# Softmax exponentials turned by 64x64 matmuls with the identity, one PSUM bank per batch element

## The chip, the cores and the metric

The kernel runs on one core of one Trainium2 chip. The metric is the device time of one execution in microseconds; lower is better. The kernel before takes 2504.32 us, the median of three runs (2503.06 to 2508.76).

## What is computed

Four layers of attention run over x, 64 batch elements of 64 tokens by 256 features, in float32. Layer 0 is a gated memory attention. Layers 1 and 3 are the same block: rotary self attention (16 heads of 16 features, causal, weights chosen per token from two experts), cross attention to a context of 64 tokens by 128 features (16 heads of 8), and a gated feed forward with two experts. Layer 2 is a latent attention (16 heads of 64, masked keys) with a GELU feed forward. What matters here is the same line in three of them:

```python
scores = jnp.einsum('bhqd,bhkd->bhqk', q * scale, k)
p = jax.nn.softmax(scores.astype(jnp.float32), axis=-1)
return jnp.einsum('bhqk,bhkd->bhqd', p, v)
```

The exponentials come out with the queries on the partitions. The product with the values contracts over the keys, so they have to be turned: keys on the partitions, for every head and batch element.

## The kernel before, in words

The 64 batch elements are worked on in 32 pairs (PAIRS). A tile `x_tile(p)` has 128 rows: 64 tokens (S) of each of the two elements of pair p. The layers are phases that follow one another. In each phase every engine has its own block with its own list of instructions, written out by hand as a loop over pairs that is shifted by one to three pairs from one step to the next. Semaphores order the engines: `x_ok.at(p + 1)` is the count at which pair p is done, and `at(p)` the count for the pair before. There is no scheduler.

PSUM is one tensor `ps_all` of eight banks of 512 columns: `ps_a`, `ps_b`, `ps_t` (0, 1, 2), `ps_s` (3 and 4), and `ps_p`, `ps_o`, `ps_d` (5, 6, 7).

For pair p, the exponentials are `probs[:, u]`, 128 partitions (64 queries of two elements) by 1024 columns (16 heads by 64 keys). In all three phases they are turned like this:

- **TensorE** makes eight transpositions of 128x128 (`probs_t` in self attention, L1005, and in cross attention, L1401; `prob_transposes` in latent attention, L551). Four go to bank `ps_p`, four to `ps_d`, and each four are announced by one step of `pt_pe`. A turned block has two heads by 64 keys on the partitions and two elements by 64 queries in the columns.
- **ScalarE** copies each bank into `pt` (`pt_copy`, L1123 and L1488; `prob_copies`, L561), 128x512 each, as soon as its own four blocks are done.
- **TensorE** multiplies with the values in `pv` (L1021 in self, L1415 in cross, L1786 in latent attention).

The order of the steps on TensorE in one round of the loop:

- self attention: scores(p), dense(p-2), probs_t(p-1), proj_qk(p+2), pv(p-1), xt_(p+3), proj_v(p+2), out_t(p-1), qk_t(p+2). The scores (L991) and pv are 64x64 float32 matmuls, and dense (L1037 to L1039) and proj_qk (L946 to L948) are full-array ones with 512 columns.
- cross attention: scores(p) (L1389, 64x64 with 512 columns), probs_t(p-1), proj_qk(p+2) (L1362, L1364), out_t(p-2) (L1423), proj_v(p) (L1376), xt_(p+3) (L1352), pv(p-1), dense(p-2) (L1431).
- latent attention: scores(p) (L1758 with a mask, then L1766: 32 matmuls of 64x64 with 64 columns, in all four quadrants of the array), half of a projection of a later group (L1720 to L1722), prob_transposes(p-1), the other half, keys (L1732 to L1734), pv(p-1), values (L1746), dense(p-1).

In cross attention ScalarE's round is pt_copy(p-1), qkt_copy(p+2) (L1480), ot_copy(p-2) (L1504), xt_copy(p+3), the two exponentials of p (L1497), and a statistic. Outputs and their transposition share bank `ps_o`, so pv(p-1) waits for ot_copy(p-2):

```python
pe.wait_ge(pt_ok.handle, pt_ok.at(p + 1))
pe.wait_ge(v_ok.handle, v_ok.at(p + 1))
if ot_ok.due(p):
    pe.wait_ge(ot_ok.handle, ot_ok.at(p))
```

Bank `ps_d` has a second user in two phases: in self attention qk_t (its copy is counted by `qkt_ok`), in latent attention dense (its reader is counted by `res_ok`).

Of the kernel before, what the change touches and what calls it, by code (L numbers as in the profile page):

```python
# [43 lines left out]
J = NH // 2  # L44
# [63 lines left out]
def build(nc, t):  # L108
    with ExitStack() as ctx:
# [421 lines left out]
        def softmax_norm(pool, sm, probs, p, u):  # L531
# [2 lines left out]
            nc.gpsimd.tensor_tensor(pr, pr, sm[:, u, 1].unsqueeze(2).broadcast_to([P, NH, S]), ALU.mult) \  # L534
                .then_inc(prob_ok.handle, 1)

        def prob_transposes(pe, probs, p, u):

            pe.wait_ge(prob_ok.handle, prob_ok.at(p + 1))
            for r, bank in enumerate((ps_p, ps_d)):  # L540

                if r == 0:
                    if pt_ok.due(p):
                        pe.wait_ge(pt_ok.handle, pt_ok.at(p))
                    if o_ok.due(p):
                        pe.wait_ge(o_ok.handle, o_ok.at(p))
                else:
                    if res_ok.due(p):
                        pe.wait_ge(res_ok.handle, res_ok.at(p))
                for j in range(4):  # L550
                    ins = nc.tensor.transpose(bank[:, j * P:j * P + P],  # L551
                                              probs[:, u, (4 * r + j) * P:(4 * r + j + 1) * P], ident)
                ins.then_inc(pt_pe.handle, 1)

        def prob_copies(act, pt, p):
            for r, bank in enumerate((ps_p, ps_d)):
                act.wait_ge(pt_pe.handle, pt_pe.at(p, r + 1))
                if r == 0:
                    if pv_pe.due(p):
                        act.wait_ge(pv_pe.handle, pv_pe.at(p))  # L560
                nc.scalar.activation(pt[:, 4 * r:4 * r + 4].rearrange("p j q -> p (j q)"), bank[:], ACT.Copy) \  # L561
                    .then_inc(pt_ok.handle, 1)


# [310 lines left out]
        def self_attention(n, loaded, load_next):  # L875
            with ExitStack() as own:
# [27 lines left out]
                pt = ob("pt", [P, J, P])  # L904
# [11 lines left out]
                with nc.Block() as block:  # L916
# [10 lines left out]
                    def _(pe):  # L927
# [67 lines left out]
                                ins.then_inc(s_pe.handle, 1)  # L995

                        def probs_t(p):
                            for r, bank in enumerate((ps_p, ps_d)):
                                pe.wait_ge(exp_ok.handle, exp_ok.at(p, r + 1))
                                if r == 0 and on_ok.due(p):  # L1000
                                    pe.wait_ge(on_ok.handle, on_ok.at(p))
                                if r == 1:
                                    pe.wait_ge(qkt_ok.handle, qkt_ok.at(min(p + 3, PAIRS)))
                                for j in range(4):
                                    ins = nc.tensor.transpose(bank[:, j * P:j * P + P],  # L1005
                                                              probs[:, p % 2, (4 * r + j) * P:(4 * r + j + 1) * P], ident)
                                ins.then_inc(pt_pe.handle, 1)

                        def pv(p):

                            pe.wait_ge(pt_ok.handle, pt_ok.at(p + 1))
                            wait_slot(pe, p)
                            if o_ok.due(p):
                                pe.wait_ge(o_ok.handle, o_ok.at(p))
                            for j in range(J):
                                at = 4 * (j % 4 // 2) + 2 * (j // 4) + j % 2
                                for h in range(2):
                                    rows = slice(S * h, S * h + S)
                                    for b in range(2):
                                        v = (v_own if b == h else v_swap)[rows, p % VS, 2 * j + h]  # L1020
                                        ins = nc.tensor.matmul(o_at[b * S:b * S + S, h, j], pt[rows, at, b * S:b * S + S], v,  # L1021
                                                               start=True, stop=True, skip_group_check=True)
                            ins.then_inc(pv_pe.handle, 2)

# [49 lines left out]
                    def _(act):  # L1074
# [43 lines left out]
                        def pt_copy(p):  # L1118
                            for r, bank in enumerate((ps_p, ps_d)):
                                act.wait_ge(pt_pe.handle, pt_pe.at(p, r + 1))  # L1120
                                if r == 0 and pv_pe.due(p):
                                    act.wait_ge(pv_pe.handle, pv_pe.at(p))
                                nc.scalar.activation(pt[:, 4 * r:4 * r + 4].rearrange("p j q -> p (j q)"), bank,  # L1123
                                                     ACT.Copy).then_inc(pt_ok.handle, 1)

                        def out_high(p):
# [183 lines left out]
        def cross_attention(n, loaded, load_next):  # L1310
            with ExitStack() as own:
# [18 lines left out]
                pt = ob("pt", [P, J, P])  # L1330
# [5 lines left out]
                with nc.Block() as block:  # L1336
# [9 lines left out]
                    def _(pe):  # L1346
# [46 lines left out]
                                ins.then_inc(s_pe.handle, 1)  # L1393

                        def probs_t(p):
                            for r, bank in enumerate((ps_p, ps_d)):
                                pe.wait_ge(exp_ok.handle, exp_ok.at(p, r + 1))
                                if pt_ok.due(p):
                                    pe.wait_ge(pt_ok.handle, pt_ok.at(p - 1, r + 1))
                                for j in range(4):  # L1400
                                    ins = nc.tensor.transpose(bank[:, j * P:j * P + P],  # L1401
                                                              probs[:, p % 2, (4 * r + j) * P:(4 * r + j + 1) * P], ident)
                                ins.then_inc(pt_pe.handle, 1)

                        def pv(p):

                            if p == 0:
                                pe.wait_ge(cold.handle, cold.at(0, 2))
# [4 lines that stand above are left out]
                            for j in range(J):  # L1413
                                for b in range(2):
                                    ins = nc.tensor.matmul(ps_o[b * S:b * S + S, j * 2 * HV:(j + 1) * 2 * HV],  # L1415
                                                           pt[:, j, b * S:b * S + S],
                                                           vb[:, p % 2, b, j].rearrange("p h d -> p (h d)"),
                                                           start=True, stop=True, skip_group_check=True)
                            ins.then_inc(pv_pe.handle, 2)
# [39 lines left out]
                    def _(act):  # L1459
# [23 lines left out]
                        def pt_copy(p):  # L1483
                            for r, bank in enumerate((ps_p, ps_d)):
                                act.wait_ge(pt_pe.handle, pt_pe.at(p, r + 1))
                                if r == 0 and pv_pe.due(p):
                                    act.wait_ge(pv_pe.handle, pv_pe.at(p))
                                nc.scalar.activation(pt[:, 4 * r:4 * r + 4].rearrange("p j q -> p (j q)"), bank,  # L1488
                                                     ACT.Copy).then_inc(pt_ok.handle, 1)

                        def exp_(p):
# [148 lines left out]
        def latent_attention(loaded, load_next):  # L1640
            with ExitStack() as own:
# [23 lines left out]
                pt = ob("pt", [P, J, P])  # L1665
# [25 lines left out]
                with nc.Block() as block:  # L1691
# [9 lines left out]
                    def _(pe):  # L1701
# [71 lines left out]
                        def pv(p):  # L1773
# [6 lines left out]
                            for r, bank in enumerate((ps_o, ps_p)):  # L1780
                                for j in range(4):
                                    for b in range(2):
                                        for h in range(2):
                                            rows = slice(S * h, S * h + S)
                                            at = (2 * j + r) * HD2
                                            ins = nc.tensor.matmul(  # L1786
                                                bank[rows, j * P + b * S:j * P + b * S + S],
                                                vb[p % 2][b][rows, at:at + HD2],
                                                pt[rows, 4 * r + j, b * S:b * S + S], start=True, stop=True,
                                                skip_group_check=True)  # L1790
                                ins.then_inc(pv_pe.handle, 1)

# [809 lines left out]
```

## Time and profile before

| | |
|---|---|
| median of three runs | 2504.32 us |
| the profiled execution | 2509.57 us |
| its span, first to last instruction | 2507.8 us |
| busy: TensorE (PE), its weight loads (PEld) | 2311.2 us (92%), 1890.0 us (75%) |
| busy: VectorE, ScalarE, GpSimd | 1410.7 us (56%), 1143.7 us (46%), 653.1 us (26%) |
| mean granted TensorE clock | 0.960 of 2.4 GHz |

A busy time is that of one engine, and engines overlap, so the column doesn't add up to the span. TensorE's instructions also overlap each other: a group's time is best read from the start of its first instruction to the start of the next group. "A <-B" names what is written and what is read, and "xN" the number of records merged into a row. PE is the matmul, PEld the load of its stationary operand, DVE is VectorE, ACT ScalarE, POOL GpSimd.

### The profile page before, as it was taken

The page shows a single profiled execution, that of the slowest core. Times are in us where ns is not written, and L with a number is a line of the kernel's source. Part 1 is how long each engine was busy: PE and PEld are TensorE (multiplying, and loading weights), DVE is VectorE, ACT ScalarE, POOL GpSimd, SP SyncE. Part 2 cuts the span into 40 slices and gives each one's busy share as a digit, 9 for nine tenths or more (in the row PEclk, how much of TensorE's full clock was granted, in tenths as well). Part 3 has the DMA queues.
Part 4 walks back from the last instruction along what each step waited for, and adds up shares of the span by engine and source line. Part 5 has one row for each costly group of instructions (what it writes and reads, how often), then busy time and mean ns, then how long its engine had stood idle before and what let it go on. Part 6 is the DMA issues. An engine that isn't in the chain of part 4 may idle for free. (4 is left out here: it accounts for less than half of the span.)

```text
span 2507.8 us, 63604 instructions
## 1 busy us (share of the span) xinstructions
PE 2311.2 (92%) x24286; PEld 1890.0 (75%) x24287; DVE 1410.7 (56%) x2866; ACT 1143.7 (46%) x2585; POOL 653.1 (26%) x833
## 2 busy tenths in 40 slices
PE   5994999997996999799999997998999998997998
PEld 4673788875765999688888876996888875666998
DVE  3563666664775333466666655554666665764433
ACT  2553444443664333334344344445444435664332
POOL 1333222212662222111111110001222214652222
PEclk9996999997998999899999998998999998998999
DMA  5440000002003111300000001000000002001111
GB/s 179 58 58 9 18 15 15 15 15 71 27 27 93 55 58 57 110 2 2 2 2 2 2 2 35 0 0 14 15 15 15 15 13 79 27 30 51 59 59 42
DMA packets 78468, 85.55 MB, mean 34 GB/s; under 512 B 19891, under 2 KB 69376, under 8 KB 78112
## 3 DMA queue, kind: packets, MB, share of 16 engines
q1 hardware_dynamic: 56016, 41.55, 7.3%
q10 hardware_dynamic: 13856, 19.61, 2.4%
q0 software_dynamic: 8368, 21.15, 2.4%
q8 instruction: 168, 2.75, 0.5%
q14 instruction: 60, 0.49, 0.1%
HBM read 52.22 MB, written 21.40 MB: 29 GB/s over the span
## 5 line engine op out<-in xcount | busy, mean ns | idle before, releaser
L1184 POOL TENSOR_TENSOR s_kx<-s_qkt,const 128x512 f32<-128x512 f32 x128 | 131.7, 1049 | 447.3 <-ACT s_qkt L1115 447.3
L2150 PE MATMUL ps_all<-f_wh,f_xh 128*128 x396 | 155.2, 392 | 10.6 <-DVE f_xl L2295 10.6
L1536 POOL TENSOR_TENSOR c_kx<-c_qkt,const 128x512 f32<-128x512 f32 x128 | 130.5, 1037 | 118.2 <-ACT c_qkt L1480 118.0
L534 POOL TENSOR_TENSOR a_probs<-a_probs,a_sm 128x1024 f32<-128x1024 f32 x32 | 60.9, 1902 | 384.6 <-DVE a_sm L529 384.6
L1123 ACT ACTIVATE s_pt<-ps_all 128x512 f32<-128x512 f32 x128 | 69.7, 594 | 186.9 <-PE ps_all L1005 186.9
L2151 PE MATMUL ps_all<-f_wh,f_xl 128*128 x396 | 149.3, 377 | 0.0
L2152 PE MATMUL ps_all<-f_wl,f_xh 128*128 x396 | 149.2, 377 | 0.0
L1874 ACT ACTIVATE self_w<-ps_all,a_q_bias 128x256 f32<-128x256 f32 x128 | 53.7, 470 | 196.5 <-PE ps_all L1722 196.5
L2290 DVE SCALAR_TENSOR_TENSOR f_h<-ps_all,rstd,f_act_g 128x688 f32<-128x688 f32 x66 | 61.6, 934 | 143.9 <-PE ps_all L2152 131.9
L2175 PE MATMUL ps_all<-f_dh,f_hh 128*128 x396 | 116.9, 295 | 4.0 <-DVE f_hl L2305 4.0
L505 DVE TENSOR_REDUCE s_mx<-ps_all 128x8 f32<-128x512 f32 x128 | 82.5, 686 | 61.3 <-PE ps_all L991 61.3
L2213 ACT ACTIVATE f_act_g<-ps_all,rstd 128x688 f32<-128x688 f32 x66 | 55.2, 837 | 132.6 <-PE ps_all L2152 132.6
L2218 ACT ACTIVATE f_hh<-ps_all 128x768 fp32r<-128x768 f32 x66 | 53.6, 812 | 132.8 <-PE ps_all L2160 132.8
L946 PE MATMUL ps_all<-s_wh,s_xh 128*128 128x512 f32 x256 | 107.2, 419 | 6.6 <-DVE s_xl L1215 6.6
L2177 PE MATMUL ps_all<-f_dl,f_hh 128*128 x396 | 111.5, 282 | 0.0
L1230 DVE TENSOR_TENSOR s_roped<-ps_all,rope 128x512 f32<-128x512 f32 x64 | 44.3, 692 | 119.5 <-PE ps_all L948 119.5
L2176 PE MATMUL ps_all<-f_dh,f_hl 128*128 x396 | 111.3, 281 | 0.0
L1585 DVE TENSOR_REDUCE c_mx<-ps_all 128x8 f32<-128x512 f32 x128 | 82.5, 686 | 44.9 <-PE ps_all L1389 44.7
L1488 ACT ACTIVATE c_pt<-ps_all 128x512 f32<-128x512 f32 x128 | 69.5, 595 | 82.6 <-PE ps_all L1401 82.6
L1097 ACT ACTIVATE s_xh<-ps_all 128x512 fp32r<-128x512 f32 x64 | 38.3, 598 | 143.1 <-PE ps_all L934 143.1
L947 PE MATMUL ps_all<-s_wl,s_xh 128*128 128x512 f32 x256 | 101.4, 396 | 0.0
L948 PE MATMUL ps_all<-s_wh,s_xl 128*128 128x512 f32 x256 | 101.0, 395 | 0.0
(322 smaller groups left out, 7518.7 us busy)
## 6 DMA issues: line engine op xcount, KB each, us to landing
s_v_swap<-s_v_own SPq DMA_DIRECT2D x128, 68.0 KB, 2.0
f_x_in<-x_sorted SPq DMA_DIRECT2D x66, 128.0 KB, 2.0
x_res<-x_sorted SPq DMA_DIRECT2D x66, 128.0 KB, 2.1
x_sorted<-x_res POOLq DMA_DIRECT2D x1, 4224.0 KB, 16.5
l_rows<-in_x SPq DMA_DIRECT2D x32, 128.0 KB, 3.6
x_res<-in_x SPq DMA_DIRECT2D x32, 128.0 KB, 7.4
x_res<-x_back SPq DMA_DIRECT2D x1, 3584.0 KB, 20.5
l_rows<-in_ctx SPq DMA_DIRECT2D x32, 64.0 KB, 4.3
```

The lines of the kernel that those rows point to most:

```text
L505: nc.vector.tensor_reduce(mx[:, u, half(r)], s3[:, half(r)], op=ALU.max, axis=AX.X) \
L946: nc.tensor.matmul(ps_a[:], xh[:, u, c, e], wh[:, k, 0:2 * D], start=(k == 0), stop=False)
L947: nc.tensor.matmul(ps_a[:], xh[:, u, c, e], wl[:, k, 0:2 * D], start=False, stop=False)
L948: ins = nc.tensor.matmul(ps_a[:], xl[:, u, c, e], wh[:, k, 0:2 * D], start=False, stop=(k == 2 * CH - 1))
L1184: ins = nc.gpsimd.tensor_tensor(kx[:, p % 2, c], qkt[:, p % 2, 2 + c].rearrange("p (b k) -> p b k", b=2).unsqueeze(2) .broadcast_to([P, 2, ...
L1536: ins = nc.gpsimd.tensor_tensor(kx[:, p % 2, b], qkt[:, p % 2, 1, b * S:b * S + S].unsqueeze(1).broadcast_to([P, RH, S]), const[:, C_H8X:C ...
L2150: nc.tensor.matmul(bank, x_high, wh[:, w_at], start=(c == 0), stop=False)
L2151: nc.tensor.matmul(bank, x_low, wh[:, w_at], start=False, stop=False)
L2152: ins = nc.tensor.matmul(bank, x_high, wl[:, w_at], start=False, stop=(c == CH - 1))
L2175: nc.tensor.matmul(bank, high, dh[:, w_at], start=(m == 0), stop=False)
L2176: nc.tensor.matmul(bank, low, dh[:, w_at], start=False, stop=False)
L2177: ins = nc.tensor.matmul(bank, high, dl[:, w_at], start=False, stop=(m == IC - 1))
```

## The change

The eight transpositions of a pair become 32 matmuls with the identity, each of 64 partitions by 64 columns. They are written once, in a new function that all three phases call:

```diff
+        def turn_probs(pe, probs, p, u):
+
+            for k in range(2):
+                if k == 1:
+                    pe.wait_ge(exp_ok.handle, exp_ok.at(p, 2))
+                for j in range(4 * k, 4 * k + 4):
+                    for h in range(2):
+                        for b, bank in enumerate((ps_p, ps_d)):
+                            rows = slice(S * b, S * b + S)
+                            ins = nc.tensor.matmul(bank[S * h:S * h + S, j * S:j * S + S],
+                                                   probs[rows, u, j * P + h * S:j * P + h * S + S], ident[rows, rows],
+                                                   start=True, stop=True, skip_group_check=True)
+            ins.then_inc(pt_pe.handle, 2)
```

Bank `ps_p` now holds element 0 of the pair and `ps_d` element 1, each with all heads, so neither bank is complete before the last four matmuls. `pt_pe` takes its two steps at once, at the end. All waits for free banks stand ahead of the first matmul. In cross attention:

```diff
                         def probs_t(p):
-                            for r, bank in enumerate((ps_p, ps_d)):
-                                pe.wait_ge(exp_ok.handle, exp_ok.at(p, r + 1))
-                                if pt_ok.due(p):
-                                    pe.wait_ge(pt_ok.handle, pt_ok.at(p - 1, r + 1))
-                                for j in range(4):
-                                    ins = nc.tensor.transpose(bank[:, j * P:j * P + P],
-                                                              probs[:, p % 2, (4 * r + j) * P:(4 * r + j + 1) * P], ident)
-                                ins.then_inc(pt_pe.handle, 1)
+                            pe.wait_ge(exp_ok.handle, exp_ok.at(p, 1))
+                            if pt_ok.due(p):
+                                pe.wait_ge(pt_ok.handle, pt_ok.at(p))
+                            turn_probs(pe, probs, p, p % 2)
```

The same is done in self attention, where the wait for `qkt_ok` moves from the fifth transposition to the front, and in latent attention, where the wait for `res_ok` does. The tile `pt` changes from `[P, J, P]` to `[P, 2, J, S]` (J is 8): the copy of bank r writes `pt[:, r]`, and the products read `pt[rows, b, at]`, `pt[:, b, j]` and `pt[rows, b, 4 * r + j]`, again 64 adjacent columns. The copies keep their number and size, and nothing else changes.

TensorE's list in cross attention, one round from the scores to the values' product, before (`ps_all` is PSUM, `c_probs` the exponentials, `const` holds the identity):

```order
L1389 MATMUL ps_all<-c_kx,c_qkt 64x512 [waits sub_ok,kx_ok]
L1389 MATMUL ps_all<-c_kx,c_qkt 64x512 x3
L1401 MATMUL ps_all<-const,c_probs 128x128 [waits pt_ok,exp_ok]
L1401 MATMUL ps_all<-const,c_probs 128x128 x3
L1401 MATMUL ps_all<-const,c_probs 128x128 [waits pt_ok,exp_ok]
L1401 MATMUL ps_all<-const,c_probs 128x128 x3
L1362 MATMUL ps_all<-c_xt,c_wq 128x128 [waits qkt_ok,xt_ok]
```

And the same piece after the change:

```order
L1391 MATMUL ps_all<-c_kx,c_qkt 64x512 [waits sub_ok,kx_ok]
L1391 MATMUL ps_all<-c_kx,c_qkt 64x512 x3
L546 MATMUL ps_all<-const,c_probs 64x64 [waits pt_ok,exp_ok]
L546 MATMUL ps_all<-const,c_probs 64x64 x15
L546 MATMUL ps_all<-const,c_probs 64x64 [waits exp_ok]
L546 MATMUL ps_all<-const,c_probs 64x64 x15
L1364 MATMUL ps_all<-c_xt,c_wq 128x128 [waits qkt_ok,xt_ok]
```

The group stands where it stood, between the scores and the projection. Eight calls have become 32, and nothing has moved past anything else. In self attention the group stands between dense and proj_qk and in latent attention between the two halves of the projection, as before.

## Rows read from the trace of the kernel before

**Rows 1.** Three stretches: length, busy PE, PEld, DVE, ACT, POOL (records), clock, DMA share, GB/s

```profile
300.00:550.00 250.00, 250.00 (x3134) 201.40 (x3132) 166.32 (x337) 121.32 (x277) 56.80 (x64) 1.00 0.06 15
620.00:750.00 130.00, 130.00 (x1665) 90.95 (x1664) 93.63 (x200) 90.02 (x223) 84.26 (x89) 1.00 0.08 26
1080.00:1440.00 360.00, 358.54 (x5229) 298.62 (x5231) 226.91 (x428) 146.05 (x300) 58.61 (x51) 1.00 0.01 2
```

**Rows 2.** Groups of instructions by line: records, busy us, mean ns, idle before

```profile
L1766 PE MATMUL ps_all<-a_kt,self_w 64*64 64x64 f32 x2048 | 37.4, 222 | 0.0
```

**Rows 3.** Timeline of PE, latent scores: start us, us, engine, line, op, out<-in, records

```profile
1254.04 1.16 PE L1766 MATMUL ps_all<-a_kt,self_w 64*64 64x64 f32 x64
1255.14 0.39 PE L1720 MATMUL ps_all<-a_xh,a_qh 128*128 128x256 f32 x1
1255.36 0.28 PE L1721 MATMUL ps_all<-a_xl,a_qh 128*128 128x256 f32 x1
```

**Rows 4.** Timeline of PE, latent attention, the values' product

```profile
1273.96 2.08 PE L1786 MATMUL ps_all<-a_pt,a_vb 64*64 64x64 f32 x64
```

**Rows 5.** Timeline of PE, latent attention, around the transpositions and the values' product

```profile
1256.55 0.28 PE L1722 MATMUL ps_all<-a_xh,a_ql 128*128 128x256 f32 x1
...
1257.66 0.28 PE L1721 MATMUL ps_all<-a_xl,a_qh 128*128 128x256 f32 x1
...
1259.56 0.28 PE L1734 MATMUL ps_all<-a_ch,a_kl 128*128 128x256 f32 x1
1259.76 0.27 PE L1786 MATMUL ps_all<-a_pt,a_vb 64*64 64x64 f32 x2
```

**Rows 6.** Timeline of ACT, copies of the turned blocks, latent and self attention

```profile
1257.60 1.08 ACT L561 ACTIVATE a_pt<-ps_all 128x512 f32<-128x512 f32 x2
...
406.94 1.09 ACT L1123 ACTIVATE s_pt<-ps_all 128x512 f32<-128x512 f32 x2 [2.90 <-PE ps_all L1005]
```

**Rows 7.** Timeline of PE, self attention, around the transpositions

```profile
406.08 0.40 PE L1039 MATMUL ps_all<-s_oh,s_otl 128*128 128x512 f32 x1
...
407.42 0.40 PE L947 MATMUL ps_all<-s_wl,s_xh 128*128 128x512 f32 x1
```

**Rows 8.** Timeline of PE, self attention, into and out of 64x64 groups

```profile
404.81 0.50 PE L1037 MATMUL ps_all<-s_oh,s_oth 128*128 128x512 f32 x1
405.14 0.39 PE L1038 MATMUL ps_all<-s_ol,s_oth 128*128 128x512 f32 x1
...
409.69 0.39 PE L948 MATMUL ps_all<-s_wh,s_xl 128*128 128x512 f32 x1
410.01 0.23 PE L1021 MATMUL ps_all<-s_v_own,s_pt 64*64 64x17 f32 x1
```

**Rows 9.** Timeline of PE and DVE, one round of cross attention

```profile
679.41 0.66 PE L1389 MATMUL ps_all<-c_kx,c_qkt 64*64 64x512 f32 x4
...
679.89 0.61 PE L1389 MATMUL ps_all<-c_kx,c_qkt 64*64 64x512 f32 x4
680.43 1.09 PE L1401 MATMUL ps_all<-const,c_probs 128*128 128x128 f32 x8
...
680.53 0.69 DVE L1585 TENSOR_REDUCE c_mx<-ps_all 128x8 f32<-128x512 f32 x1 [0.26 <-PE ps_all L1389]
...
681.36 0.61 PE L1362 MATMUL ps_all<-c_xt,c_wq 128*128 128x128 f32 x4
...
682.98 0.30 PE L1415 MATMUL ps_all<-c_vb,c_pt 128*64 128x18 f32 x4
```

**Rows 10.** Timeline of ACT, the same round of cross attention

```profile
681.12 1.08 ACT L1488 ACTIVATE c_pt<-ps_all 128x512 f32<-128x512 f32 x2 [1.28 <-PE ps_all L1401]
...
682.51 0.27 ACT L1504 ACTIVATE c_ot<-ps_all 128x128 f32<-128x128 f32 x1
```

**Rows 11.** Timeline of ACT and PE, a late round of cross attention

```profile
760.70 0.28 ACT L1504 ACTIVATE c_ot<-ps_all 128x128 f32<-128x128 f32 x1
...
761.13 0.26 PE L1415 MATMUL ps_all<-c_vb,c_pt 128*64 128x18 f32 x3 [0.51 <-ACT c_ot L1504]
```

More of the change, by code:

```diff
@@ L535, in softmax_norm @@
                 .then_inc(prob_ok.handle, 1)
+        def turn_probs(pe, probs, p, u):
[10 more added lines that the diff above has]
+            ins.then_inc(pt_pe.handle, 2)
         def prob_transposes(pe, probs, p, u):
             pe.wait_ge(prob_ok.handle, prob_ok.at(p + 1))
-            for r, bank in enumerate((ps_p, ps_d)):
-                if r == 0:
-                    if pt_ok.due(p):
[L544 to L549, printed above, removed]
-                for j in range(4):
-                    ins = nc.tensor.transpose(bank[:, j * P:j * P + P],
-                                              probs[:, u, (4 * r + j) * P:(4 * r + j + 1) * P], ident)
-                ins.then_inc(pt_pe.handle, 1)
+            if pt_ok.due(p):
+                pe.wait_ge(pt_ok.handle, pt_ok.at(p))
+            if o_ok.due(p):
+                pe.wait_ge(o_ok.handle, o_ok.at(p))
+            if res_ok.due(p):
+                pe.wait_ge(res_ok.handle, res_ok.at(p))
+            turn_probs(pe, probs, p, u)
         def prob_copies(act, pt, p):
@@ L560, in prob_copies @@
                         act.wait_ge(pv_pe.handle, pv_pe.at(p))
-                nc.scalar.activation(pt[:, 4 * r:4 * r + 4].rearrange("p j q -> p (j q)"), bank[:], ACT.Copy) \
+                nc.scalar.activation(pt[:, r].rearrange("p j q -> p (j q)"), bank[:], ACT.Copy) \
                     .then_inc(pt_ok.handle, 1)
@@ L903, in self_attention @@
                 probs = ob("probs", [P, 2, NH * S])
[L904 removed]
+                pt = ob("pt", [P, 2, J, S])
                 on = ob("on", [P, D])
@@ L997, in probs_t @@
                         def probs_t(p):
-                            for r, bank in enumerate((ps_p, ps_d)):
-                                pe.wait_ge(exp_ok.handle, exp_ok.at(p, r + 1))
[L1000 to L1005, printed above, removed]
-                                                              probs[:, p % 2, (4 * r + j) * P:(4 * r + j + 1) * P], ident)
-                                ins.then_inc(pt_pe.handle, 1)
+                            pe.wait_ge(exp_ok.handle, exp_ok.at(p, 1))
+                            if on_ok.due(p):
+                                pe.wait_ge(on_ok.handle, on_ok.at(p))
+                            pe.wait_ge(qkt_ok.handle, qkt_ok.at(min(p + 3, PAIRS)))
+                            turn_probs(pe, probs, p, p % 2)
                         def pv(p):
@@ L1020, in pv @@
                                         v = (v_own if b == h else v_swap)[rows, p % VS, 2 * j + h]
-                                        ins = nc.tensor.matmul(o_at[b * S:b * S + S, h, j], pt[rows, at, b * S:b * S + S], v,
+                                        ins = nc.tensor.matmul(o_at[b * S:b * S + S, h, j], pt[rows, b, at], v,
                                                                start=True, stop=True, skip_group_check=True)
@@ L1395, in probs_t @@
                         def probs_t(p):
-                            for r, bank in enumerate((ps_p, ps_d)):
-                                pe.wait_ge(exp_ok.handle, exp_ok.at(p, r + 1))
-                                if pt_ok.due(p):
-                                    pe.wait_ge(pt_ok.handle, pt_ok.at(p - 1, r + 1))
[L1400 to L1403, printed above, removed]
+                            pe.wait_ge(exp_ok.handle, exp_ok.at(p, 1))
+                            if pt_ok.due(p):
+                                pe.wait_ge(pt_ok.handle, pt_ok.at(p))
+                            turn_probs(pe, probs, p, p % 2)
                         def pv(p):
@@ L1788, in pv @@
                                                 vb[p % 2][b][rows, at:at + HD2],
-                                                pt[rows, 4 * r + j, b * S:b * S + S], start=True, stop=True,
+                                                pt[rows, b, 4 * r + j], start=True, stop=True,
                                                 skip_group_check=True)
```

10 lines of the change are left out of this document (5 added, 5 removed).

## The prediction

> **What bounds the kernel now.** I read the busy time by stretches first. In the steady middle of self, cross and latent attention TensorE is busy for 250.00 of 250.00, 130.00 of 130.00 and 358.54 of 360.00 us, while VectorE, the next one, is busy for 166, 94 and 227 us [rows 1]. There is no TensorE idle time in which anything could be hidden, so each nanosecond that the change adds to TensorE's own stream in these stages is paid, and so is a wait that it puts there. The next view is TensorE's timeline around one pair of each stage, with starts and not busy times, because the engine's instructions overlap: what a group costs is the time from its first start to the start of what follows. The last view is ScalarE's timeline beside it in cross attention. There the reader is to see how close the copies end before TensorE needs them.
>
> **What a 64x64 float32 matmul costs here.** The trace has the same kind already: the latent scores (L1766), 32 calls of 64 rows by 64 columns with 64 moving columns, over all four quadrants. They stand in the trace as 2048 records for 32 pairs x 32 calls, two for each call [rows 2]. A transposition is one record (8 per pair). The 64 records of a pair run from 1254.04, and the next group starts at 1255.14: 1.10 us, and the last of them ends 1.16 us after the first start [rows 3]. The latent product with the values (L1786) has as many records of the same form, but visits only two quadrants in turn, and takes 2.08 us [rows 4]. Twice the time for half the quadrants says that each quadrant takes its own next record at a fixed pace and that quadrants run side by side. The new loop (j, then h, then b) visits all four: rows by b, output partitions by h. It has them in another order than L1766 (row half alternating first, not column half), and the two row halves write two banks, as in L1766. I take L1766's body of 1.10 us.
>
> The Trainium skill, "TensorEngine Tiling (Array Packing)", section Restrictions and Gotchas, says that on trn2 column tiling can't be combined with transpose mode for float32 input. That speaks against this change: the eight one-record transpositions can't become one-record quadrant transpositions. The trace agrees as far as it goes, with two records for each 64x64 call [rows 2]. By the rule the sum is the one below; without it, it would be that of the third rival.
>
> **Latent attention, 32 pairs.** Before: from L1722 at 1256.55, the last start ahead of the transpositions, to L1721 at 1257.66, the second start behind them: 1.11 us [rows 5]. After: the entry from a full-array matmul into 64x64 ones, L1734 to L1786, 0.20 us; the body 1.10; and the first full-array matmul behind a 64x64 group, L1720 to L1721, 0.22 [rows 3, 5]. Sum 1.52, so **+0.41 us per pair, +13.1 us**. Cover: ScalarE's copies a_pt end at 1258.68 and the product starts at 1259.76. They will start when the second bank is full, not the first: 1256.55 + 0.20 + 1.16 + 0.04 = 1257.95 in place of 1257.60, 0.35 us later against TensorE's own 0.41, so the 1.08 us of slack stay [rows 5, 6]. The wait for res_ok, now ahead of the whole group, is for a residual of the pair before, two groups of matmuls ago.
>
> **Self attention, 2 x 32 pairs.** Before: L1039 at 406.08 to L947 at 407.42, 1.34 us. After: entry from a 512-wide matmul 0.32 (409.69 to 410.01), body 1.10, first 512-wide one behind 64x64 ones 0.33 (404.81 to 405.14) [rows 7, 8]. Sum 1.75, **+0.41 us per pair, +26.2 us**. Cover: the copies s_pt end at 408.03 and L1021 starts at 410.01 [rows 6, 8]. They will start at 406.08 + 0.32 + 1.16 + 0.04 = 407.60 in place of 406.94, 0.66 us later where 1.98 are free, with proj_qk in between. The qkt_ok wait, formerly ahead of the fifth transposition, is for a copy of the previous round. ScalarE's exponential behind the copies is as much later, and is needed a round later. Both cost nothing.
>
> **Cross attention, 2 x 32 pairs.** This stage differs twice. First, what runs ahead of the transpositions is already 64x64 (L1389). Its two batches of four start at 679.41 and 679.89, and L1401 at 680.43. Of the 0.48 between the batches about 0.05 is the start itself (0.66 against 0.61 us of length), so a quadrant is free about 0.43 us after 679.89. I let the new group start at 680.32, 0.11 earlier than L1401 [rows 9]; the bound on the other side is no gain at all. Then 1.10 in place of 0.93 for the body (680.43 to 681.36), and about 0.05 more for the first full-array step behind it (a term between nothing and the 0.10 of latent attention). So TensorE's own stream would bring it to L1415 at 682.98 - 0.11 + 0.17 + 0.05 = 683.09, **+0.11 us**.
>
> Second, ScalarE. pv waits for pt_ok, v_ok and ot_ok, and ot_copy stands behind both pt copies and qkt_copy on ScalarE. Today the pt copies start at 681.12, when the first bank is done, and ot_copy runs from 682.51 to 682.78 [rows 10]. Late in the stage, where proj_qk is gone and TensorE does wait, L1415 starts at 761.13, 0.15 after the end of ot_copy at 760.98 [rows 11]. In the steady part the release therefore comes at 682.93, only 0.05 us before TensorE is there. With the change, pt_pe counts both banks after the last matmul, at 680.32 + 1.16 = 681.48. VectorE starts 0.03 us after such an end (680.50 to 680.53) [rows 9], so ScalarE starts near 681.52, 0.40 later, with the same work behind it: ot_copy ends at 683.18, and pv starts at 683.33 in place of 683.09. A wait of 0.24 us appears in every pair, and the period grows by 683.33 - 682.98 = **0.35 us, 64 x 0.35 = 22.4 us**. Queued behind the waiting pv on TensorE are dense and the next scores, so nothing gives it back. The later qkt copy delays kx on GpSimd by 0.4 us, needed two rounds later; the exponential also ends about 0.4 later, and its reader, the next transpositions, stands behind pv, dense and the next scores. Neither costs.
>
> Nothing changes on the DMA queues, and the other copies keep size and number. In 1080 to 1440, 300 to 550 and 620 to 750 us the granted clock is 1.00, the 2.4 GHz level [rows 1]; TensorE stays as busy, so I price nothing for the clock.
>
> **Sum:** 13.1 + 26.2 + 22.4 = 61.7 us. The profiled execution took 2509.57 us (span 2507.8) and would take 2571. It lies 5.25 above the median of the runs, 2504.32; onto that median, **2566.0 us**.
>
> **Rivals.** A change within 0.2%, 5 us, can't be told from none in this kernel.
> (1) *The order of the quadrants keeps them from running side by side.* The new loop changes the row half with each call, and nothing in the trace has exactly this sequence. L1786, which also changes the row half each time, takes 2.08 us for 64 records [rows 4]. With that body each pair pays 0.92 more, 160 x 0.92 = 147 us: 2713. For it: no row shows the sequence. Against: L1786 changes to a quadrant with another column half, and only two of them take part, which explains its pace without the order. The Trainium skill, "TensorE: Matmul & The Clock Gate", section Packing small matmuls, says that matmuls start and end strictly in program order. By that rule a call's second record holds back all other quadrants and this rival would be right, but L1766's 1.10 us, half of L1786's, disagrees.
> (2) *Cross attention has no new wait*: the release is earlier than I reckon, or the stream slower in front of it. Then cross costs 0.11 x 64 = 7.0 and the sum is 46.3: 2550.6. It stands or falls with 0.2 us, and belongs to my range.
> (3) *Faster: an identity matmul stays one record.* This decides if the new calls appear 32 times a pair in the trace, not 64. Batches of four come 0.058 us apart (1.10 us less some 0.16 for the end, over 16), so eight fewer take 0.47 off the body. Self and latent then give 0.41 - 0.47 = -0.06 x 96 = -6, cross 0.35 - 0.47 = -0.12 x 64 = -8: 2490.8. For it: the old transposition, also float32 against the identity, is one record. Against: every 64x64 call of the trace is two.
> (4) *The extra work is hidden*, within 0.2%. It needs TensorE idle time, which rows 1 deny.
>
> **Chances.** Forecast with rival (2): 0.83. Rival (1): 0.09. Rival (3): 0.05. No change: 0.03. The range is that of the forecast's unknowns. Low end: no wait in cross (-15.4) and no dearer entry or exit than before (about 0.1 of the 0.41, 96 x 0.1 = 10): 2540. High end: no earlier start in cross (+0.11 x 64 = 7), 0.1 us more at each mode change (160 x 0.1 = 16), and some 3 us in the last pairs of each stage, where the values' product already waits for the copies: 2592. Both rivals (1) and (3) lie outside, 0.14 together. Faster 0.05, same 0.03, slower 0.92.
>
> **What would show it.** In the profile after: the new line with 64 records a pair; body 1.10 us from first start to the next group; rounds longer by 0.41 us in self and latent and by 0.35 in cross; and a wait of the values' product for c_ot in nearly all pairs of cross, where today the last ones show it [rows 11]. I am wrong if the body is near 2 us, if there are 32 records, or if cross grows by 0.11 with no wait for c_ot.

## The result, and the profile after

The changed kernel takes 2567.66 us, the median of four runs (2565.05 to 2572.95), against 2505.38 for the kernel before on the same chip (2503.06 to 2508.76). The ratio is 1.025, with a 95% interval of 1.0228 to 1.0272. The two profiled executions took 2565.05 and 2509.57 us, 55.5 apart; the medians are 62.3 apart. Both figures matter below, because durations come from the profiled ones. Of all executions behind the times in this document two are set aside as slow ones, 7756 us of self_only and 2947 of before_ot_first.

Part 1 of the page after (busy us, share of the span, records):

```profile
span 2563.3 us, 81431 instructions
PE 2353.0 (92%) x33246; PEld 1921.1 (75%) x33247; DVE 1410.9 (55%) x2866; ACT 1141.0 (45%) x2585; POOL 653.7 (26%) x833
```

TensorE has 8960 records more, 160 pairs x (64 - 8) = 8960. So each of the 32 calls of a pair is two records, and the other engines do what they did. The stretches that answer to [rows 1] (length, busy PE, PEld, DVE, ACT, POOL, clock, DMA share, GB/s):

```profile
300.00:550.00 250.00, 250.00 (x4296) 196.03 (x4298) 159.76 (x323) 118.31 (x271) 54.64 (x62) 1.00 0.06 15
635.00:765.00 130.00, 129.01 (x2947) 95.64 (x2940) 89.77 (x189) 84.15 (x214) 80.06 (x83) 1.00 0.08 27
1105.00:1465.00 360.00, 358.64 (x6511) 296.50 (x6504) 221.57 (x418) 147.27 (x297) 55.88 (x48) 1.00 0.01 3
```

TensorE is as full as it was and the clock is at its 2.4 GHz level. Only in cross attention is a little of it idle now, 0.99 of 130 us. The timeline of TensorE in self attention, which answers to [rows 7] (start us, us, engine, line, op, out<-in, records; L1041, L953 and L954 are L1039, L946 and L947 of before):

```profile
421.96 0.39 PE L1041 MATMUL ps_all<-s_oh,s_otl 128*128 128x512 f32 x1
422.28 1.16 PE L546 MATMUL ps_all<-const,s_probs 64*64 64x64 f32 x64
423.37 0.50 PE L953 MATMUL ps_all<-s_wh,s_xh 128*128 128x512 f32 x1
423.71 0.39 PE L954 MATMUL ps_all<-s_wl,s_xh 128*128 128x512 f32 x1
```

The entry is 0.32, the body 1.09, the first step behind it 0.34, and the stretch 423.71 - 421.96 = 1.75 us against 1.34 before. In latent attention, for [rows 5]:

```profile
1312.91 0.28 PE L1720 MATMUL ps_all<-a_xh,a_ql 128*128 128x256 f32 x1
1313.12 1.16 PE L546 MATMUL ps_all<-const,a_probs 64*64 64x64 f32 x64
1314.21 0.39 PE L1718 MATMUL ps_all<-a_xh,a_qh 128*128 128x256 f32 x1
1314.43 0.28 PE L1719 MATMUL ps_all<-a_xl,a_qh 128*128 128x256 f32 x1
```

1.52 us against 1.11. And one round of cross attention, TensorE, for [rows 9]:

```profile
694.49 1.09 PE L1391 MATMUL ps_all<-c_kx,c_qkt 64*64 64x512 f32 x8
695.40 1.11 PE L546 MATMUL ps_all<-const,c_probs 64*64 64x64 f32 x64
696.44 0.71 PE L1364 MATMUL ps_all<-c_xt,c_wq 128*128 128x128 f32 x4
696.99 0.39 PE L1366 MATMUL ps_all<-ctx_all,c_w_kv 128*128 128x128 f32 x2
...
697.79 0.44 PE L1354 MATMUL ps_all<-const,x_res 128*128 128x128 f32 x2
698.25 1.11 PE L1413 MATMUL ps_all<-c_vb,c_pt 128*64 128x18 f32 x32
...
699.92 0.66 PE L1391 MATMUL ps_all<-c_kx,c_qkt 64*64 64x512 f32 x4
```

with ScalarE's side of it, for [rows 10]:

```profile
696.57 1.09 ACT L1486 ACTIVATE c_pt<-ps_all 128x512 f32<-128x512 f32 x2 [1.77 <-PE ps_all L546]
697.54 0.39 ACT L1478 ACTIVATE c_qkt<-ps_all 128x256 f32<-128x256 f32 x1
697.81 0.30 ACT L1502 ACTIVATE c_ot<-ps_all 128x128 f32<-128x128 f32 x1
```

Counted from the start of the scores, the new group starts 0.91 us in (1.02 before), the projection 1.95 in, as before, and the values' product 3.76 in (3.57). The product starts 0.14 after the end of ot_copy (698.11). This round is 5.43 us; the scores start again at 716.32, four rounds on, so one of four is longer and the mean is 21.83 / 4 = 5.46. Before it was 20.98 / 4 = 5.245 (a scores group at 679.41 and one at 700.39).

```profile
716.32 0.66 PE L1391 MATMUL ps_all<-c_kx,c_qkt 64*64 64x512 f32 x4
```

Four more rows of the kernel before are used below: the same round of cross attention on TensorE and ScalarE, and the scores four rounds on.

```profile
681.80 0.39 PE L1364 MATMUL ps_all<-ctx_all,c_w_kv 128*128 128x128 f32 x2
682.61 0.44 PE L1352 MATMUL ps_all<-const,x_res 128*128 128x128 f32 x2
...
682.23 0.38 ACT L1480 ACTIVATE c_qkt<-ps_all 128x256 f32<-128x256 f32 x1
...
700.39 0.66 PE L1389 MATMUL ps_all<-c_kx,c_qkt 64*64 64x512 f32 x4
```

The three differences, 0.41 x 64 + 0.41 x 32 + 0.21 x 64 = 26.2 + 13.1 + 13.4 = 52.8 us, account for all but 3 of the 55.5 us between the profiled executions. They are the steady rounds. The first and last rounds of a phase differ from them: from the first to the last group of turned exponentials of each phase, self attention is 28.0 us longer, cross attention 15.1 and latent attention 13.7 (the first self attention, for one, from 260.75 to 577.39 before and from 260.10 to 591.22 after), together 56.8.

One thing has to be known before differences of a few us are read: the time of an execution follows its mean granted clock. Of the 43 executions of the kernel before that ran beside the experiments, the three at 0.966 took 2502.5 to 2504.3 us and the two at 0.959 took 2510.4 and 2510.6. That is about 1 us for each 0.001, an estimate from these five. The profiled execution before stood at 0.960 and the one after at 0.965, so at an equal clock they would lie some 60 apart and not 55.5.

### The profile page after: what moved, and what is told of

Same layout as the page of the kernel before. It is cut to its first block and busy times, and to the rows that moved or that the text cites. A ratio compares the mean times of both kernels' runs of the same rounds, so it can differ in the third digit from the quotient of the medians.

```text
span 2563.3 us, 81431 instructions
## 1 busy us (share of the span) xinstructions
PE 2353.0 (92%) x33246; PEld 1921.1 (75%) x33247; DVE 1410.9 (55%) x2866; ACT 1141.0 (45%) x2585; POOL 653.7 (26%) x833
## 5 line engine op out<-in xcount | busy, mean ns | idle before, releaser
L2288 DVE SCALAR_TENSOR_TENSOR f_h<-ps_all,rstd,f_act_g 128x688 f32<-128x688 f32 x66 | 61.7, 935 | 142.8 <-PE ps_all L2150 131.2
L953 PE MATMUL ps_all<-s_wh,s_xh 128*128 128x512 f32 x256 | 108.3, 423 | 6.6 <-DVE s_xl L1217 6.6
L954 PE MATMUL ps_all<-s_wl,s_xh 128*128 128x512 f32 x256 | 101.9, 398 | 0.0
L2303 DVE TENSOR_TENSOR f_hl<-ps_all,f_hh 128x768 fp32r<-128x768 f32 x66 | 63.2, 958 | 65.5 <-ACT f_hh L2216 65.5
```

Source lines behind the costliest of these rows:

```text
L953: nc.tensor.matmul(ps_a[:], xh[:, u, c, e], wh[:, k, 0:2 * D], start=(k == 0), stop=False)
L954: nc.tensor.matmul(ps_a[:], xh[:, u, c, e], wl[:, k, 0:2 * D], start=False, stop=False)
```

## Experiments

The first theory was that the cost is TensorE's own stream plus a wait in cross attention; its rivals stand in each expectation. Ratios are against the kernel before, run on the same chip.

**The three parts alone.** Each is the kernel before with the change in one phase:

```diff
                         def probs_t(p):
-                            for r, bank in enumerate((ps_p, ps_d)):
...
+                            turn_probs(pe, probs, p, p % 2)
```

> The change in self attention alone. Theory A (the cost is TensorE's own stream, pair by pair: +0.42 us for each of 64 pairs, from a body of 1.09 in place of 0.79 us and dearer entry and exit): +27 us on before, rounds of 10.81 us in both self attentions, every other phase as before. Rival B (a program-wide cost of 18,000 more TensorE instructions to fetch, 238 in place of 168 packets on the instruction queue): less than 27 in self attention, and the rest spread over phases that were not touched.

> The change in cross attention alone. Theory A: +0.22 us for each of 64 pairs, +14 us, rounds of 5.44 us: TensorE itself reaches the values' product 0.10 later, and waits 0.09 more for ot_copy. The prediction's own term was +0.35, +22.4 us. Rival B: more than 14, part of it outside cross attention.

> The change in latent attention alone. Theory A: +0.42 us for each of 32 pairs, +13.4 us, and nothing elsewhere. With self (27) and cross (14) the three add up to 54 to 56, which is the difference of the two profiled executions (55.5). Rival B: the three single changes add up to clearly less or more than the whole.

Measured: self attention alone 2539.92 us, ratio 1.0138 (1.0117 to 1.0158); cross alone 2525.68, 1.0082 (1.0065 to 1.0099); latent alone 2521.78, 1.0062 (1.0045 to 1.0078); before 2504.04. The spans of the profiled executions are 2539.4, 2521.2 and 2521.3, that is 31.6, 13.4 and 13.5 over 2507.8, together 58.5 against 55.5 for the whole. By the spans, cross and latent match the expectation; self is 5 above it, though its rounds are 10.81 us as expected (10.39 before) and the stretch in it is no longer than in the changed kernel:

```profile
421.91 0.39 PE L1048 MATMUL ps_all<-s_oh,s_otl 128*128 128x512 f32 x1
422.23 1.16 PE L546 MATMUL ps_all<-const,s_probs 64*64 64x64 f32 x64
423.32 0.50 PE L960 MATMUL ps_all<-s_wh,s_xh 128*128 128x512 f32 x1
```

(entry 0.32, body 1.09). The phases that self_only doesn't touch keep their length: the two cross attentions take 159.75 and 159.76 us from first to last group (159.75 and 159.77 before), latent attention 431.78 (431.78 before). So there is no fetching cost spread over them, and rival B falls.

Some of the 5 us can be found. The last rounds of a phase have less work, and whether TensorE's clock has fallen to its 1.2 GHz level there differs from execution to execution. In the second self attention the last round but one is 10.59 us in self_only and 7.76 in the changed kernel, and a 512-wide matmul takes 0.63 us in the one, at a granted clock of 0.50 from 2082 to 2086 us, and 0.40 in the other, at 1.00. Windows of self_only and of the changed kernel (length, busy PE, PEld, DVE, ACT, POOL, clock, DMA share, GB/s), and the matmul ahead of the group in each:

```profile
2078.00:2086.00 8.00, 6.85 (x90) 4.26 (x90) 3.34 (x7) 1.68 (x4) 0.00 (x0) 0.60 0.01 2
2085.97 0.63 PE L1048 MATMUL ps_all<-s_oh,s_otl 128*128 128x512 f32 x1
```

```profile
2098.00:2105.00 7.00, 4.96 (x116) 3.25 (x111) 3.72 (x9) 2.51 (x5) 0.00 (x0) 1.00 0.01 2
2104.56 0.40 PE L1041 MATMUL ps_all<-s_oh,s_otl 128*128 128x512 f32 x1
```

The medians put the three at 35.9, 21.6 and 17.7, a sum of 75 against 62 for the whole, and the intervals of the first two (29 to 40 and 16 to 25) don't reach down to the expected 27 and 14. The clock accounts for much of it. self_only's executions all stood at 0.959, and those of the kernel before at 0.963 on average. With means in place of medians, against all 43 executions before and at 1 us for each 0.001, the parts cost 30, 19 and 14 us, together 63, and the whole change 62. That is an estimate, but by it the three parts add up to the whole. Each is still 1 to 6 us above what its rounds give, and that rest is not located.

**The wait in cross attention.** ot_copy is put ahead of qkt_copy on ScalarE, in the changed kernel and, as a control, in the kernel before:

```diff
-                            if has(p + 2):
-                                qkt_copy(p + 2)
                             if has(p - 2):
                                 ot_copy(p - 2)
+                            if has(p + 2):
+                                qkt_copy(p + 2)
```

> The changed kernel, with ot_copy ahead of qkt_copy on ScalarE in cross attention. Theory A (in cross attention pv waits for ot_copy, which the late pt copies hold back): the release comes some 0.3 us earlier, TensorE no longer waits, rounds of 5.34 in place of 5.44 us, 64 x 0.1 = 6 us less than the change. Rival C (the whole 0.22 us of cross attention is TensorE's own stream, the wait is only apparent): rounds of 5.44, same time as the change.

> The kernel before with ot_copy ahead of qkt_copy in cross attention, the control of the same swap in the changed kernel. Theory A (before the change pv is released 0.05 us before TensorE gets there, so nothing waits): same time as before within 0.2%, rounds of 5.25 us. Rival C: if it gains 6 us here too, the swap does something else than to remove the new wait.

Measured: 2561.34 us, ratio 1.0228 (1.0209 to 1.0247), 6.3 below the changed kernel's median, which would not do by itself, since the two intervals overlap; the control 2504.59, 0.9992 (0.9982 to 1.0002), no difference, with rounds of 5.24 to 5.25 us as before. The rounds decide. TensorE and ScalarE in the changed kernel with the swap:

```profile
700.61 1.09 PE L1391 MATMUL ps_all<-c_kx,c_qkt 64*64 64x512 f32 x8
...
703.92 0.44 PE L1354 MATMUL ps_all<-const,x_res 128*128 128x128 f32 x2
704.28 1.11 PE L1413 MATMUL ps_all<-c_vb,c_pt 128*64 128x18 f32 x32
...
705.96 1.09 PE L1391 MATMUL ps_all<-c_kx,c_qkt 64*64 64x512 f32 x8
```

```profile
702.84 1.08 ACT L1486 ACTIVATE c_pt<-ps_all 128x512 f32<-128x512 f32 x2 [1.79 <-PE ps_all L546]
703.81 0.28 ACT L1502 ACTIVATE c_ot<-ps_all 128x128 f32<-128x128 f32 x1
```

The product now starts 0.36 after L1354, as before the change (682.98 - 682.61 = 0.37), and not 0.46; every steady round is 5.35. So 0.09 us of each round (0.18 of every fourth, see below) was the wait for ot_copy, and the rest of cross attention's cost is TensorE's own. Rival C falls. In the changed kernel the product starts 0.14 us after the end of ot_copy in every pair but the first, as the kernel before does only in the last ones, where it waits [rows 11]; in the steady rounds of before it is 0.20.

**The order of the quadrants.**

```diff
-                    for h in range(2):
-                        for b, bank in enumerate((ps_p, ps_d)):
+                    for b, bank in enumerate((ps_p, ps_d)):
+                        for h in range(2):
```

> The changed kernel with the two inner loops of turn_probs swapped, so that the column half alternates first, as in the latent scores. Theory A (each quadrant takes its own next record every 0.058 us, whatever the order of the calls): body 1.09 us, time as the changed kernel within 0.2%. Rival D (the order matters, by the row group that a weight load may overtake): body measurably longer or shorter, at least 5 us on the whole.

Measured: 2571.18 us, 1.0251 (1.0234 to 1.0268) against 1.025 for the change. The bodies are those of the changed kernel, 1.09 us in self and latent attention and 1.04 in cross. The order has no part in it, and rivals D and (1) fall.

**Two quadrants at a time.**

```diff
+            pe.wait_ge(exp_ok.handle, exp_ok.at(p, 2))
+            for d in range(2):
+                for j in range(8):
+                    for b, bank in enumerate((ps_p, ps_d)):
+                        h = (b + d) % 2
```

> The changed kernel with turn_probs in two passes over the heads, each over one diagonal of two quadrants. Theory A: only two quadrants work at a time, so the 64 records need 32 steps of 0.058 in place of 16: body about 2.02 us, +0.93 on each of 160 pairs, about +149 us on the changed kernel. Rival D (records go one after another, 0.015 us each, whatever the quadrant): no difference.

The wait for the second exponentials now stands ahead of both passes. It costs nothing: in cross attention the group still starts 0.41 us after the matmul ahead of it.

Measured: 2688.76 us, 1.0712 (1.0695 to 1.073), 121 above the changed kernel.

```profile
1389.09 1.91 PE L545 MATMUL ps_all<-const,a_probs 64*64 64x64 f32 x64
1390.93 0.39 PE L1717 MATMUL ps_all<-a_xh,a_qh 128*128 128x256 f32 x1
```

The body is 1.84 us, 0.75 more than 1.09, and 0.75 x 160 = 120. The same 64 records take longer when they visit two quadrants at a time: a quadrant takes its records one by one, and the four run side by side. The 2.02 that I expected was too much. I took it from L1786, which alternates the same two quadrants to the end, while here the second pass uses the two that the first leaves idle. Read one by one, the starts show what that gives: the records start two by two every 0.058 us up to 1389.85, four by four for three steps, and two by two again from 1390.07. So the second pass begins three steps, 0.17 us, before the first is done, which is the 0.18 that was missing.

**Half rows, in transpose mode.** 16 transpositions of 64 rows by 128 columns, which leave the same blocks in the same banks:

```diff
-                    for h in range(2):
...
+                    for b, bank in enumerate((ps_p, ps_d)):
+                        rows = slice(S * b, S * b + S)
+                        ins = nc.tensor.transpose(bank[:, j * S:j * S + S], probs[rows, u, j * P:(j + 1) * P],
+                                                  ident[rows, rows])
```

> The changed kernel with 16 true transpositions of 64 rows by 128 columns a pair in place of the 32 matmuls: same banks, same layout, same late announcement, but one record a call and no column halves. Theory A (a weight load of 128 columns paces a call at 0.109 us, and two row halves run side by side): body about 0.79 us as before the change, rounds of self attention 10.39 to 10.5 us, whole kernel 2505 to 2515 us, a little over before in cross attention through the late announcement. Rival E (row halves don't run side by side): 16 x 0.109 = 1.74 us, +0.95 a pair on before, about 2660 us.

Measured: 2506.61 us, ratio 0.9998 (0.9988 to 1.0008).

```profile
1311.38 0.28 PE L1718 MATMUL ps_all<-a_xh,a_ql 128*128 128x256 f32 x1
1311.59 0.71 PE L545 MATMUL ps_all<-const,a_probs 64*128 64x64 f32 x16
1312.23 0.39 PE L1716 MATMUL ps_all<-a_xh,a_qh 128*128 128x256 f32 x1
1312.45 0.29 PE L1717 MATMUL ps_all<-a_xl,a_qh 128*128 128x256 f32 x1
```

and the eight full transpositions of the kernel before, in the pair of [rows 5]:

```profile
1256.67 1.04 PE L551 MATMUL ps_all<-const,a_probs 128*128 128x128 f32 x8
1257.46 0.36 PE L1720 MATMUL ps_all<-a_xh,a_qh 128*128 128x256 f32 x1
```

One record a call, and the body is 0.64 us, less than the 0.79 (1256.67 to 1257.46) of the full ones. I had expected 0.79, from a step of 0.109 us, and the step is 0.063. Rival E falls with it. The stretch is 1.07 us against 1.11 before, and the rounds are 10.41, 5.12 and 14.17 us in self, cross and latent attention (10.39, 5.245 and 14.19 before). So without the doubled records the same banks and the same late announcement cost next to nothing. The Trainium skill, "TensorEngine Tiling (Array Packing)", section Restrictions and Gotchas, bars transpose mode for float32 only with column tiling, and this form, which splits the rows alone, keeps it.

**Half rows, as plain matmuls.** Against half_rows:

```diff
-                        ins = nc.tensor.transpose(bank[:, j * S:j * S + S], probs[rows, u, j * P:(j + 1) * P],
-                                                  ident[rows, rows])
+                        ins = nc.tensor.matmul(bank[:, j * S:j * S + S], probs[rows, u, j * P:(j + 1) * P],
+                                               ident[rows, rows], start=True, stop=True,
+                                               skip_group_check=True)
```

> half_rows with plain matmuls against the identity in place of the transpositions: 16 calls a pair of 64 rows by 128 columns, no column halves, but not in transpose mode. Theory A (the two records that a plain float32 call takes are what the change pays for, not the column halves): 32 records a pair, 16 steps of about 0.06 us, body about 1.1 us as in the changed kernel, self rounds near 10.81 us, 2555 to 2570 us. Rival F (the split into column halves costs, not the records): 16 records or a body near 0.64 us, 2505 to 2510 us.

Measured: 2720.9 us, ratio 1.0852 (1.0831 to 1.0873). Both expectations missed.

```profile
1407.93 2.00 PE L545 MATMUL ps_all<-const,a_probs 64*128 64x64 f32 x32
1409.86 0.39 PE L1717 MATMUL ps_all<-a_xh,a_qh 128*128 128x256 f32 x1
```

There are 32 records, as theory A said, but the body is 1.93 us, not 1.1. So leaving transpose mode costs twice: two records for one, and longer steps. With some 0.15 for the end (an estimate), 16 steps give (1.93 - 0.15) / 16 = 0.111 us a step for the plain form with 128 stationary columns, (1.09 - 0.15) / 16 = 0.059 for the 64-column form of the change, and (0.64 - 0.15) / 8 = 0.061 for transpose mode with 128. Read one by one, the starts are 0.112, 0.058 and 0.063 us apart behind a somewhat longer first step. What leaves transpose mode costs 1.29 us (0.64 to 1.93); the column halves then give 0.84 of it back. Rival F had the sign wrong: the halves don't cost, they save.

**Half rows where they pay.** The kernel before with the half-row transpositions in cross attention alone, and then also in latent attention and with ot_copy ahead of qkt_copy:

> The kernel before with the 16 half-row transpositions in cross attention alone. Theory A: rounds of 5.12 us there in place of 5.25, 64 x 0.125 = 8 us less than before, 2496 to 2499 us, faster than both kernels. Rival G (half_rows as a whole measured as before, so the shorter rounds are given back at the ends of the phases): 2503 to 2507 us.

> The kernel before with the half-row transpositions in cross and latent attention, and ot_copy ahead of qkt_copy in cross attention. Theory A: cross rounds lose the wait for ot_copy that half_rows shows (the product starts 0.14 us after it), about 0.06 us more, so 5.06 us; latent rounds 0.03 us shorter: 64 x 0.185 + 32 x 0.03 = 13 us less than before, 2492 to 2495 us. Rival G: 2503 to 2507 us.

Measured: 2501.11 us, ratio 0.9979 (0.997 to 0.9988), and 2498.16 us, ratio 0.997 (0.996 to 0.9981), before 2506.38. Both are faster than both kernels, the one before by 5.3 and 8.2 us, 0.2 and 0.3%. half_cross has rounds of 5.12 us there, as expected. TensorE in the second:

```profile
700.41 1.11 PE L1416 MATMUL ps_all<-c_vb,c_pt 128*64 128x18 f32 x32
701.45 0.70 PE L1432 MATMUL ps_all<-c_w_out,c_ot 128*128 128x256 f32 x2
702.08 1.09 PE L1394 MATMUL ps_all<-c_kx,c_qkt 64*64 64x512 f32 x8
703.10 0.71 PE L545 MATMUL ps_all<-const,c_probs 64*128 64x64 f32 x16
703.74 0.71 PE L1367 MATMUL ps_all<-c_xt,c_wq 128*128 128x128 f32 x4
...
705.47 1.11 PE L1416 MATMUL ps_all<-c_vb,c_pt 128*64 128x18 f32 x32
```

The round is 5.06 us, as expected, 0.19 below 5.245, and 64 x 0.19 = 12 us. The span is 2494.0, 13.8 below before; the medians show 8.2. The first and last rounds of a phase gain less than the others: from first to last group the two cross attentions together are 6.4 us shorter in half_cross, not 8, and 10.4 in half_cl_ot, not 12, and latent attention gains 0.1 and not 1. At an equal clock, estimated as above, the two runs are 5.7 and 8.9 us faster than before and half_rows, whose executions stood at 0.959 on average, 3. So rival G as it stood (no gain) falls, and some 1 to 2 us are left open.

## Why the prediction was right, and where a term was off

The forecast was 2566.0 with a range of 2540 to 2592, and 2567.66 was measured. Point by point:

- **TensorE is full in these stages, and each added nanosecond is paid.** Right. It is as busy after, in the stretches that answer to [rows 1], and each part alone lengthens its own rounds and no others.
- **Two records a call, body as of L1766.** Right: 64 records, 1.09 us against the 1.10 taken. The third rival (one record) falls with the count, the first (order of the quadrants) with the body and with cols_first. The Trainium skill, "TensorE: Matmul & The Clock Gate", section Packing small matmuls, has matmuls start strictly in program order. By that a call's second record would hold back the next call whatever its quadrant, and two_quads and the change would take the same time; they take 1.84 and 1.09 us.
- **Latent +0.41, self +0.41 a pair.** Right to the hundredth: 1.52 for 1.52, 1.75 for 1.75. The covers held: the copies for the values' product stay ahead of it.
- **Cross +0.35 a pair.** This term was mis-sized: 0.21 measured, 13.4 us for 22.4. The entry was right, 0.11 earlier. The body is 1.04, not 1.10: behind other 64x64 work the group has no start of its own to pay (its second four records start 0.056 us after the first four, in latent attention 0.107). The first full-array step behind it costs 0.10 more (696.99 - 696.44 = 0.55 for four records against 0.44), not 0.05. These two errors cancel. What was wrong is the release: "ScalarE starts near 681.52, 0.40 later, with the same work behind it". It started 0.37 later in its round (696.57 - 694.49 = 2.08 against 1.71), but the work behind it was not a queue. qkt_copy started at 682.23 not because the pt copies ended at 682.20 but because the projection L1364 ended at 682.19 (681.80 + 0.39); with the pt copies later, qkt_copy and ot_copy close up behind them, each starting before the one ahead has ended (697.54 against 696.57 + 1.09 = 697.66). ot_copy ends 3.62 into the round against 3.37, 0.25 later and not 0.40, and the wait is 0.09 and not 0.24. So the mechanism was right, shown by after_ot_first and its control, and the wait was 0.15 too large.
- **The check that I named for it was half wrong.** I expected the view of waits to name c_ot in nearly all pairs. It still names it 8 times. The idle time before the product is counted from the end of L1354, which overlaps the wait; only the starts show it, 0.46 after L1354 against 0.37.
- **The sum.** 61.7 us predicted, 62.3 between the medians, 55.5 between the profiled executions and some 60 between those at an equal clock. The rounds account for 52.8 of it. The prediction's 61.7 are these 52.8 and the cross term's 9 too many; the medians' 62.3 are the same 52.8, 4 more from the first and last rounds of the phases, and some 5 that are not located. That the forecast sits 1.7 us from the measured median is luck: a term that was 9 us too large stands in for some 9 that the sum has no term for.

Left open: in cross attention every fourth round of the changed kernel is 0.09 us longer (5.53 for 5.44), because ScalarE starts its copies that much later after the last matmul, 0.16 us in place of 0.07. With ot_copy first the copies are late in every fourth round too, the one at 700.61 among them, but the product no longer waits for them and the rounds stay equal. With the half-row transpositions the copies always start 0.04 after. No view names what holds them.

## What to carry to other kernels

A float32 transposition against the identity is cheap only in transpose mode. Halving its rows kept that here. Quadrants that halve the columns too are plain matmuls with two records a call (no run tries transpose mode on a column half), and four quadrants side by side don't make up for that (1.09 us against 0.79 for eight full transpositions and 0.64 for sixteen half-row ones). Price an operation by a row of the same shape, type and quadrants, and count the entry and the exit between tile shapes; and before shifting a queue of copies as a block, ask of each one whether it follows the copy ahead of it or waits for another engine, since the second kind absorbs the shift.

## What the runs showed of the hardware that I hadn't expected

- In transpose mode two row halves run side by side, and 16 calls of 64x128 take less (0.64 us) than 8 of 128x128 (0.79). A step is 0.063 us with 64 moving columns; the full ones start 0.109 us apart.
- A plain float32 record with 128 stationary columns takes 0.112 us a step where transpose mode takes 0.063 for as many (both with 64 rows and 64 moving columns). The Trainium skill, "TensorE: Matmul & The Clock Gate", section LDWEIGHTS, says that a weight load goes by its columns alone, columns / 1.2 in ns: 107 and 53 ns for 128 and 64. The two plain forms come near (112 and 58), the half-row transposition with 63 ns for 128 columns doesn't.
- Into a group of another tile shape the step is 0.21 us where it is 0.12 between full-array ones: 1313.12 - 1312.91 and, with 64x128 transpositions, 1311.59 - 1311.38, against 1256.67 - 1256.55 before. Out of it, the first full-array step depends on what stands there. In latent attention it is 0.22 behind either shape, but it was 0.20 behind the eight full transpositions (1257.66 - 1257.46), so the shape adds only 0.02; in cross attention it is 0.21 and was 0.11.
- Each quadrant goes on by itself: two_quads starts its second pass on two idle quadrants while the first still runs on the other two, four records to a step and not two.
- The time of this kernel goes with the mean granted clock of the execution, by about 1 us for each 0.001 (2502.5 to 2504.3 us at 0.966, 2510.4 and 2510.6 at 0.959). A gain of 3 us, as in half_rows, is lost in it.
